# Second layer's attention: sums turned in the odd half, divided on VectorE; copies, statistics and norms moved

## What is computed

```
xn = layernorm(x);  x = x + attention0(xn) + ffn0(xn)   # 16 heads of 64; 32 experts, 6 taken
xn = layernorm(x);  x = x + attention1(xn) + ffn1(xn)   # below
```

## Time and profile before

| what | value |
|---|---|
| median of 3 runs | 1156.31 us (1155.72 to 1156.43) |
| the profiled execution | 1155.76 us |
| its span, first to last instruction | 1154.0 us |
| TensorE clock granted | 1.00 of full speed in every stage |
| second layer, group one / group two | about 939 to 1045 / 1045 to 1151 us of the span |
| rounds 1 to 4 of group one begin at | about 987, 1001.6, 1015.6 and 1029.9 us |
| rounds 1 to 4 of group two begin at | about 1092, 1106.2, 1120.3 and 1134.1 us |

### The profile page before, as it was taken

One profiled execution on the slowest core, in us unless ns is written; L12 is line 12 of the kernel. 1 busy time (PEld: TensorE's weight loads), 2 busy tenths in 40 slices (PEclk: granted clock), 3 DMA queues, 4 the chain that ended last, 5 costly groups with the idle time before them and its releaser, 6 DMA issues.

```text
span 1154.0 us, 24229 instructions
## 1 busy us (share of the span) xinstructions
PE 1139.0 (99%) x8984; PEld 897.8 (78%) x8984; DVE 998.3 (87%) x1917; ACT 839.7 (73%) x2240; POOL 484.9 (42%) x423
## 2 busy tenths in 40 slices
PE   8999999999999999999999999999999999999998
PEld 6778877877777787777778777877787767777776
DVE  7989798979897989898979897998888878898897
ACT  6886777577767775777577757776777757877886
POOL 2337600770077006700670067006750577735841
PEclk9999999999999999999999999999999999999999
DMA  8004101410041003101320032003300320000001
GB/s 270 2 32 145 49 1 31 138 57 1 31 139 55 1 31 129 66 1 31 129 65 1 25 129 71 2 18 129 119 1 9 136 87 1 2 21 19 2 11 28
DMA packets 44965, 63.93 MB, mean 55 GB/s; under 512 B 8240, under 2 KB 19120, under 8 KB 44592
## 3 DMA queue, kind: packets, MB, share of 16 engines
q1 hardware_dynamic: 44848, 62.39, 16.4%
HBM read 59.48 MB, written 2.88 MB: 54 GB/s over the span
## 4 chain that ended last, share of the span: by engine, by line
PE 90%; DVE 5%; ACT 2%; issue 1%; SPq 0%; DMA 0%; POOL 0%; DVEq 0%; ACTq 0%; POOLq 0%
PE psum L1730 14%; PE psum L1749 13%; PE psum L65 13%; PE psum L67 12%; PE psum L66 12%; PE psum L1671 11%; PE psum L1684 2%; PE psum L1696 2%; PE psum L2003 2%; PE psum L1753 1%; DVE mneg L1304 1%; PE psum L2059 1%; PE psum L1615 1%; ACT probs L876 1%; PE psum L2077 1%
## 5 line engine op out<-in xcount | busy, mean ns | idle before, releaser
L834 ACT ACTIVATE probs<-psum,mneg 128x256 f32<-128x256 f32 (+3 forms) x400 | 187.5, 486 | 109.6 <-DVE mneg L1285 109.0
L1730 PE MATMUL psum<-ident,probs 128*128 128x128 f32 x1600 | 210.1, 276 | 3.8 <-ACT probs L876 3.5
L1285 DVE TENSOR_REDUCE mneg<-psum 128x2 f32<-128x1024 f32 (+3 forms) x256 | 194.5, 818 | 21.4 <-PE psum L1684 17.5
L1276 DVE COPY pt<-psum 128x512 f32<-128x512 f32 x256 | 164.8, 683 | 41.5 <-PE psum L1730 39.5
L1730 PEld LDWEIGHTS psum<-ident,probs 128*128 128x128 f32 x1600 | 177.9, 141 | 28.4 <-ACT probs L834 8.2
L577 POOL TENSOR_TENSOR rstd<-var,mhalf 128x4 f32<-128x4 f32 x7 | 7.1, 1013 | 335.4 <-DVE var L1167 335.4
L1749 PE MATMUL psum<-pt,v_all 128*64 128x384 f32 (+5 forms) x1088 | 142.6, 412 | 0.0
L1749 PEld LDWEIGHTS psum<-pt,v_all 128*64 128x64 f32 (+1 forms) x1088 | 69.7, 135 | 62.7 <-issue 50.2
L65 PE MATMUL psum<-xt_hi,gu_hi 128*128 128x512 f32 x272 | 110.2, 405 | 0.0
L1363 DVE TENSOR_TENSOR sg<-sg,crow 128x512 f32<-128x512 f32 x88 | 106.1, 1206 | 3.6 <-DMA crow<-weights 0.9
L67 PE MATMUL psum<-xt_hi,gu_lo 128*128 128x512 f32 x272 | 107.7, 396 | 0.0
(11 more groups left out here) (307 smaller groups left out, 2895.2 us busy)
## 6 DMA issues: line engine op xcount, KB each, us to landing
crow<-weights SPq DMA_DIRECT2D x256, 128.0 KB, 2.9
rrow<-sums SPq DMA_DIRECT2D x128, 128.0 KB, 2.9
gu_raw<-in_gu SPq DMA_DIRECT2D x1, 2176.0 KB, 12.3
x_all<-in_x SPq DMA_DIRECT2D x7, 256.0 KB, 4.9
out_rows<-x_all SPq DMA_DIRECT2D x7, 256.0 KB, 2.3
down_raw<-in_down SPq DMA_DIRECT2D x1, 1088.0 KB, 13.4
wqkv_raw<-in_wqkv SPq DMA_DIRECT2D x1, 768.0 KB, 6.4
wqkv_raw<-in_wqkv SPq DMA_DIRECT2D x1, 512.0 KB, 4.0
```

The lines of the kernel that those rows point to most:

```text
L834: last = act.activation(probs[:, h * HALF + PROB[t]:h * HALF + PROB[t] + w], bank[score_bank(rnd, c) + h][:, o:o + w], ACT.Exp, bias=mneg[ ...
L1276: dve.tensor_copy(pt[:, s % 2, :, 3 - s // 2, :], turn_bank(rnd, s).rearrange("p (j q) -> p j q", q=P)).then_inc(pt_ready, 1)
L1285: last = dve.tensor_reduce(mneg_h[:, :, t], psum[:, b:b + 2, o:o + P * (t + 1)], AX, ALU.max, negate=True)
L1730: last = nc.tensor.transpose(dst[:, i * P:(i + 1) * P], probs[:, v:v + P], ident[:, :])
```

## The change

- PE: turn_sums1 moves from the end of the even half into the odd half, behind the odd pair's last scores, and into bank 7; the even pair's turn 4 goes to bank 6. output_rows moves behind turn 1 (second round) or turn 3 (third and fourth).
- DVE: in rounds two to four it divides, by multiplying the values in SBUF by the sums in bank 7 (divide), and leaves turn 2 of the even pair and turn 0 of the odd pair to ACT. In group one it takes turn 2 of the last odd pair itself again. add_attention moves behind turn 3 in the third and fourth rounds.
- ACT: the copy of the sums goes, except in the group's last batch; the two copies of turns come.
- POOL: the multiplication goes; in group one the first three normalised rows of the next group come, as a subtraction and a multiplication of 128x512 each, and the inverse roots of batches 6 and 7 stand together ahead of the first spread.
- Statistics: batch 6's on DVE go to the first layer's last batch, batch 7's to group one's first round, the first half between the copies and take_ffn, the second behind turn 1.
- Seam: turn 4 of the last odd pair is taken by DVE; PE's turn_sums1 there waits for add_attention of the third batch, no longer for turn 4's copy.

The diff, cut to its core (indentation reduced):

```diff
@@ -246,9 +246,10 @@
...
     return bank[[6, 2, 4, 3, 5][s]]
-return bank[([2, 3, 4, 7, 7] if k % (2 * G) else [6, 7, 0, 1, 7])[s]]
+return bank[([2, 3, 4, 7, 6] if k % (2 * G) else [6, 7, 0, 1, 7])[s]]
...
         SUMS = bank[5]
+        SUMS1 = bank[7]
@@ -738,6 +739,14 @@
...
 
+    def norm_rows1(g):
+        s = slice((n0 + G + g) * TILES, (n0 + G + g + 1) * TILES)
+        x = xn1[g]
+        pool.wait_ge(rows_ready, n0 + g + 1)
+        pool.wait_ge(x1_rstd_ready, n0 + G + g + 1)
+        setup.step(pool.tensor_tensor(x, x_all[:, n0 + G + g, :, :], mv[:, s, 0].unsqueeze(2).to_broadcast([P, TILES, D]), ALU.subtract))
+        pool.tensor_tensor(x, x, rstd[:, s].unsqueeze(2).to_broadcast([P, TILES, D]), ALU.mult).then_inc(row1_ready[g], 1)
+
@@ -774,14 +783,13 @@
...
         norm_qk(g)
+    if q + 1 < GROUPS:
+        inv_sqrt1(B - 2)
+        inv_sqrt1(B - 1)
...
         spread_sums1(n0 + g)
-        if q == 0 and 0 < g < G - 1:
-            inv_sqrt1(B - 3 + g)
-        if g < G - 1:
-            pool.wait_ge(rrow_ready, n0 + g + 1)
-            pool.wait_ge(y_ready, copied1(n0 + g + 1))
-            pool.tensor_tensor(y1t[g], y1t[g], rrow[:, 0, :], ALU.mult).then_inc(y_divided, 1)
+        if q + 1 < GROUPS and g:
+            norm_rows1(g - 1)
@@ -889,7 +897,7 @@
...
     act.wait_ge(y_divided, ROUNDS0 + n)
-    act.activation(rrow[:, 0, :], SUMS, ACT.Copy).then_inc(rrow_ready, 1)
+    act.activation(rrow[:, 0, :], SUMS1, ACT.Copy).then_inc(rrow_ready, 1)
@@ -1100,8 +1108,6 @@
...
             take_tile1_1(ka - 1)
-            if q == 0 and g > 1:
-                take_turned1(ka - 1, 2)
@@ -1118,13 +1124,16 @@
...
             copy_y1(g - 1)
-            take_sums1(n0 + g - 1)
-        if g:
+            take_turned1(ka, 2)
...
         exps1(kb, 1, 0)
+        if kb == 2 * B - 1:
+            take_turned1(kb, 0)
...
             take_tile1_1(ka)
+        elif kb < 2 * B - 1:
+            take_turned1(kb, 0)
@@ -1132,10 +1141,11 @@
...
             round_q(ROUNDS0 + n0 + g + 2, 1.0)
-    take_tile1_1(2 * (n0 + G) - 1)
...
         take_ht(q + 1, 0)
+    else:
+        take_tile1_1(2 * (n0 + G) - 1)
@@ -1257,8 +1267,9 @@
...
         variances0(b + 1)
-        if b:
-            add_row_stats(b - 1, x_all[:, b - 1, :, :])
+    if p == 7 and b:
+        dve.wait_ge(x1_ready, b)
+        add_row_stats(b - 1, x_all[:, b - 1, :, :])
@@ -1295,6 +1306,10 @@
...
         dve.tensor_copy(turned_rows1(k)[:, s % 2, :, 3 - s // 2, :], turn_bank1(k, s).rearrange("p (j q) -> p j q", q=P)).then_inc(pt1_ready[s], 1)
+
+def take_tile1_1(k):
+    dve.wait_ge(turned1[4], k + 1)
+    dve.tensor_copy(turned_rows1(k)[:, :, 0:2, 1, :], turn_bank1(k, 4).rearrange("p (h j q) -> p h j q", h=2, q=P)).then_inc(pt1_ready[4], 1)
@@ -1401,7 +1416,7 @@
...
             take_turned(n, [3])
-            if 0 < b < B - 1:
+            if b:
@@ -1520,6 +1535,11 @@
...
 
+    def divide(g, n0=n0):
+        dve.wait_ge(sums_turned, n0 + g + 1)
+        dve.wait_ge(y_ready, copied1(n0 + g + 1))
+        dve.tensor_tensor(y1t[g], y1t[g], SUMS1, ALU.mult).then_inc(y_divided, 1)
+
@@ -1529,8 +1549,7 @@
...
         if g:
-            if q or g == 1:
-                take_turned1(ka - 1, [2])
+            take_turned1(ka - 1, [2])
@@ -1539,10 +1558,13 @@
...
             row_maxima1(kb, 0)
-            take_turned1(ka, [1, 0, 2, 3])
+            take_turned1(ka, [1, 0, 3])
...
             take_turned1(ka, [0, 3])
+            if q == 0:
+                dve.wait_ge(x1_ready, B)
+                add_row_stats(B - 1, x_all[:, B - 1, :, :])
@@ -1552,7 +1574,9 @@
...
             invert_sums1(ka)
-        take_turned1(kb, [0])
+            take_turned1(kb, [0])
+        else:
+            divide(g - 1)
@@ -1561,18 +1585,15 @@
...
             row_maxima1(kb + 1, 0)
-        elif q + 1 < GROUPS:
-            dve.wait_ge(rows_ready, n0 + 1)
-            norm_rows1(n0 + G, 0)
-        if g:
+        if g == 1:
...
         take_turned1(kb, [1])
+        if q == 0 and g == 0:
+            sum_row_stats(B - 1, x1_var_ready)
...
         take_turned1(kb, [3])
-        if q == 0 and 0 < g < G - 1:
-            b = B - 3 + g
-            dve.wait_ge(x1_ready, b + 1)
-            row_stats(b, x_all[:, b, :, :], x1_var_ready)
+        if g > 1:
+            add_attention(g - 1)
@@ -1581,21 +1602,17 @@
...
         dve.wait_ge(y_done, ROUNDS0 + B + 1)
-        dve.wait_ge(rrow_ready, B)
+        dve.wait_ge(rrow_ready, GROUPS)
...
     take_turned1(2 * (n0 + G) - 1, [2])
-    dve.wait_ge(rows_ready, n0 + 2)
-    norm_rows1(n0 + G, 1)
-    if q + 1 < GROUPS:
-        dve.wait_ge(rows_ready, n0 + G - 1)
-        norm_rows1(n0 + G, G - 2)
-        stats1(q + 1, 0, 0)
+    take_tile1_1(2 * (n0 + G) - 1)
+    stats1(q + 1, 0, 0)
     dve.wait_ge(y_done, ROUNDS0 + n0 + G)
-    dve.wait_ge(rrow_ready, n0 + G)
+    dve.wait_ge(rrow_ready, q + 1)
@@ -1733,7 +1750,7 @@
...
     pe.wait_ge(spread_ready, n + 1)
-    transpose_rows(SUMS, spread).then_inc(sums_turned, 1)
+    transpose_rows(SUMS1, spread).then_inc(sums_turned, 1)
@@ -2066,7 +2083,7 @@
...
         elif q and g:
-            pe.wait_ge(rrow_ready, n0)
+            pe.wait_ge(rrow_ready, q)
@@ -2134,7 +2151,6 @@
...
     def output_rows(g, n0=n0):
-        pe.wait_ge(rrow_ready, n0 + g + 1)
@@ -2151,7 +2167,6 @@
...
         turn1(k, 1)
-        pe.wait_ge(pt1_ready[4], k)
@@ -2251,7 +2266,6 @@
...
         turn1(k, 2)
-        turn_sums1(n0 + g - 1)
@@ -2275,10 +2289,9 @@
...
         if g:
-            pe.wait_ge(pt1_ready[3], k)
+            pe.wait_ge(y_ready, copied1(n0 + g))
...
             pe.wait_ge(pt1_ready[2], k)
-            pe.wait_ge(rrow_ready, n0 + g)
@@ -2287,7 +2300,9 @@
...
         if g:
-            pe.wait_ge(y_ready, copied1(n0 + g - 1))
+            pe.wait_ge(pt1_ready[3], k)
+            turn_sums1(n0 + g - 1)
+            pe.wait_ge(pt1_ready[4], k)
@@ -2298,16 +2313,17 @@
...
             return
-        if g:
-            pe.wait_ge(pt1_ready[4], k)
-            output_rows(g - 1)
...
         turn1(k, 1)
+        if g == 1:
+            output_rows(g - 1)
...
         turn1(k, 3)
+        if g > 1:
+            output_rows(g - 1)
@@ -2330,7 +2346,7 @@
...
         break
-    pe.wait_ge(pt1_ready[4], 2 * (n0 + G))
+    pe.wait_ge(rows_ready, n0 + G - 1)
...
```

## The result

| what | before | after |
|---|---|---|
| median | 1156.04 us (1155.72 to 1156.69, 21 runs) | 1157.61 us (1157.06 to 1159.71, 21 runs) |
| the profiled execution, its span | 1155.76, 1154.0 us | 1157.61, 1155.8 us |
| after / before | | 1.0013, 95% interval 1.0007 to 1.0019 |

The change is slower by 1.6 us. This many runs tell the difference from zero, but it is only 0.13%, inside the 0.2% that the prediction counted as no change. The predicted time was 1156.8 us, in a range from 1153.8 to 1158.8.

The account below looks back on a forecast made before the run. PE was busy 1139.0 of 1154.0 us, DVE and ACT nearly full, ACT's slack against DVE 0.38 per round. Terms summed to +0.5: 1156.3 on the profiled execution, 1156.8 as median, range 1153.8 to 1158.8.

Parts of the forecast that it names:

- term 4: Group one's fourth round and the seam: PE's stop for DVE's normalised rows goes, POOL having them ready; -0.8 us.
- term 6: Group one's first round: batch 7's statistics delay ACT's first exponentials and, by their second half, turn 3's copy; +0.6 us.
- term 5: Group two's fourth round and end: 0.46 of sums, less 0.2 kept, plus 0.1 for the division; +0.3 us.
- Term 1: Group two's third round: ACT gates the odd scores, and its run with turn 0's copy delays the next scores; +0.1 us.
- Term 2: Group one's third round: batch 6's statistics leave DVE, turn 2's copy returns, round ends at 13.94; -0.3 us.
- Term 3: Second rounds, both groups: sums cost PE 0.46, new stop at turn 1 0.27, turn_k's stop shrinks; +0.3 us each.
- Term 7: POOL and first layer: inverse roots and spread hidden by 0.5, moved DVE work falls into idle time; no cost.
- Rival A: DVE was the bound: stops ending on it vanish with nothing late next; -3.3 us, 1153.0 us, chance 0.16.
- Rival B: ACT becomes the bound everywhere, its extra 0.48 paid five times; +2.6 us, 1158.9 us, chance 0.07.
- Rival C: First round: DVE's statistics are held beside POOL's long powers; 1.9 us added, 1158.7 us, chance 0.03.

Follow-up runs that it names:

- e2: The changed kernel plus one unused ACT copy of 128x512 behind the copy of the odd pair's turn 0, in five rounds; 1159.18 us, 1.0027.
- e6: The kernel before with only the statistics moved, both inverse roots ahead of the first spread, and turn 2 on DVE in every round; 1156.31 us, 1.0004.
- e4: The changed kernel with sums turned in the even half again and divided there by DVE, output_rows ahead of turn 1, odd pair's turn 0 on DVE; 1154.89 us.
- e7: The kernel before with only the normalised rows of the next group's first three batches on POOL; 1155.78 us, 1.0002.
- e8: e7 with the last odd pair's turn 4 copied by DVE ahead of turn 2, not by ACT; 1154.90 us, 0.9992 against the kernel before.
- e3: The changed kernel with the odd pair's turn 0 copied by DVE again, behind its division, not by ACT; 1157.19 us, 1.0012.
- e1: The changed kernel with batch 7's statistics moved into group one's feed-forward and between the first pair's copies of turns 0 and 3; 1156.38 us, 1.0004.
- e5: e4 with batch 7's statistics placed as in e1; 1154.33 us, 0.9986 against the kernel before.

## Why the prediction came out as it did

The forecast held: within 0.2%, the sign of the small rest included, and mostly for the reasons given. Two reasons were incomplete, those of term 4 and term 6. The time was 0.8 us low, and that it was not more is in part luck: the sum was set on 1156.31, the median of three runs, where 21 runs gave 1156.04. Against before, +0.5 was forecast and +1.57 and +1.10 measured in medians; by the ledger the work behind 980 us costs +1.12, so 0.6 was missing from the terms (0.26 of it in term 6, 0.15 in term 5), and what is above that varied between the two measurements of the same kernel.

**Term 1, third round, group two (+0.1): +0.12.** Step and reason held. The odd scores stand 0.24 behind ACT, and ACT's longer run decides the round's end. The traced execution was 1.29 late at the first scores of this round (1121.78 against 1120.49). Less this, ACT's run ended at 1134.16 and the next scores started at 1134.46, where 1134.19 and 1134.44 were forecast. e2 shows it from the other side, 0.52 for 0.52.

**Term 2, third round, group one (-0.3): -0.24.** e6 gives -0.39 without the longer ACT run, e2 +0.28 with one more copy.

**Term 3, second rounds (+0.3 each): +0.34 and +0.31.** The new stop ahead of turn 1 was there, and not among the waits: it lies inside a group. PE in group two's second round, against the earlier trace rows:

```profile
1116.62 0.65 PE L1632 MATMUL psum<-ident,crow 128*128 128x128 f32 x4
1117.12 1.31 PE L1747 MATMUL psum<-ident,probs 128*128 128x128 f32 x8
1118.26 1.06 PE L2157 MATMUL psum<-wo,v_all 128*128 128x128 f32 x8
1119.17 0.66 PE L1632 MATMUL psum<-ident,yt 128*128 128x128 f32 x4
...
1120.10 0.66 PE L1632 MATMUL psum<-ident,yt 128*128 128x128 f32 x4
```

Turns 0 and 1 together take 1.31, where eight matmuls without a stop take 1.04 to 1.06: 0.27, the forecast's number. turn_q stands at 1119.17 and turn_k at 1120.10; turn_k has no stop, where it had one of 0.31, or 0.47 by distances. e4, without the sums there, has +0.01.

**Term 4, the seam (-0.8): -0.72.** PE at the seam of the changed kernel, against the earlier trace rows:

```profile
1045.57 0.66 PE L1632 MATMUL psum<-ident,crow 128*128 128x128 f32 x4
1046.06 0.60 PE L1632 MATMUL psum<-ident,room 128*128 128x128 f32 x4
1046.50 0.38 PE L2018 MATMUL psum<-bias_bf,bias_on 96*128 96x512 bf16 x1
```

No stop is left. The size was right, one reason was missing: the forecast put the gain on POOL's rows, and e7 gives them nothing. The gain also needs turn 4's copy off ACT, which the forecast only priced as harmless. That the sum came right is luck in this point: the change does both. The seam itself is worth 1.04 (e8); the difference to 0.72 is what the fourth round loses, 0.25 of it to turn 0's copy on ACT (e3: -0.97).

**Term 5, fourth round of group two and end (+0.3): +0.45.** The forecast's own parts, 0.46 - 0.2 + 0.1, add up to 0.36 and were written as 0.3. PE in that round of the changed kernel:

```profile
1142.00 0.29 PE L1701 MATMUL psum<-hide,later 64*128 64x128 bf16 x4 [0.19 <-DVE pt L1308]
...
1144.53 0.66 PE L1632 MATMUL psum<-ident,crow 128*128 128x128 f32 x4
...
1145.98 1.16 PE L2157 MATMUL psum<-wo,room 128*128 128x128 f32 x8
```

The execution was 1.41 late at this round's first scores and 1.22 late at the masks of 1142.00 (1140.78 in before): 0.19 of the sums' place is kept, as forecast, and the stop for DVE's copy is what takes the rest. The sums then take 0.49 (to the next turn at 1145.02), and output_rows, which meets the division, takes 0.99 to the next turn at 1146.97, against 0.90 in before. The remaining 0.06 is spread over steps of 0.01 to 0.03. So each part was about right, and what was missing is the rounding and these small steps. e4, with +0.01, shows that all of it hangs on the sums' place and the edits that go with it.

**Term 6, first round (+0.6): +0.86.** The largest miss, in a term whose place was right: e6 and e1 show that the statistics are its whole cause. Its path was incomplete and one size too small. "The next maximum is late by only 0.4" was right: ACT began that chunk at 998.25, in before at 997.12, which is 0.39 more than the 0.74 by which this execution was late already. But the first exponentials, late by the whole 0.9, also gate PE's turns: they start at 998.22 against 996.57, 0.91 late, DVE's copy of a turn behind them is 0.87 late (999.32 against 997.71), and with it all that DVE does afterwards. DVE's idle time of 0.49 ahead of its inversion at 1000.58 in before then took part of the second half, which was 0.78 and not 0.56: 0.21 of this is in one instruction, nmean, 0.38 against the 0.17 of the same line at 981.12 in e1. e1 moved both halves at once, so how the 0.86 divides between them isn't shown.

**Term 7, POOL and first layer (0): held in size.** The spread of the second round was hidden, but by 1.0 and not by the 0.5 forecast: it ended at 1009.22 and DVE's inversion stood at 1010.24. The condition named, that without the first round's half microsecond DVE's next maxima would slip, did not come true: in e1 that cover is gone, the spread ended at 1008.43, the inversion stood at 1008.70 without a stop, and the round is +0.30 as in the changed kernel. What e5 met is another wait, which only the sums in the even half have: 0.54 of PE's time, ahead of the turn of the sums. The first layer costs nothing that can be seen: 0.05 and -0.05 at 980 us in the second trace of the changed kernel and in e1.

**Rival A** (DVE was the bound, -3.3) was right that DVE's stops at the ends of the odd halves, at turn_k and at the seam go, and fell as the forecast said: ACT was next at once. At the ends of the even halves DVE got six new stops. **Rival B** (ACT everywhere, +2.6) holds for the third rounds and group one's fourth, where one more copy came back whole (e2: 0.52, 0.52 and 0.50); the second rounds gave back half of it. **Rival C** (POOL holds the statistics, +1.9) fell: the first half took 0.86, beside a multiplication of two SBUF tensors on POOL and then beside the first of two powers of 2.27 each. The row that spoke against C was weak evidence, since POOL's copy lay beside only the first 0.2 of its 0.86. What was held was a small neighbour of theirs, for 0.21.

The lower end of the terms' own bounds, added by half, is 1155.45 and not 1155.2; nothing else was worked out from it.

## What to carry to other kernels

Where three queues are each over 80% full, what an instruction costs is decided by its place and not by its engine: the same sums, with the edits that go with them, cost 0.3 to 0.5 us a round in one half and nothing in the other (e4 against the changed kernel), and a copy moved between ACT and DVE changed the total by 0.1 us. Before an edit, look for the hole that it is to fill, and ask which of the other queues is within 0.3 us of being last; afterwards lay the two traces against each other instruction by instruction, since a stop can hide in a longer group. When one edit takes a delay away, look at what that delay had covered.

## What the runs showed of the hardware

A DVE tensor_scalar of four elements per partition took 0.38 us in the first round, beside POOL's multiplication of two SBUF tensors, and ended at 1002.44, as that one did (two of them from 1001.21 for 1.20: 1002.41). It did the same in e4 (0.41, ending at 1001.95, POOL's at 1001.93) and in e6 (0.39, ending at 1002.17, POOL's at 1002.15). In e1 the same line took 0.17 beside a POOL instruction as small as itself (981.05, 0.20), and for batch 7 it took 0.27, ending at 993.44 with a POOL multiplication that ended at 993.41. The Trainium skill (SBUF — State Buffer, section "SBUF: two separate sides") says that VectorE and GpSimd share a port pair which one of them holds for a whole instruction while the other waits. The trace agrees, and shows it for an instruction of this size: priced by its own length it is too cheap by the rest of POOL's.

The statistics were not slowed: 0.86 at 994.83, as in the earlier trace rows. POOL's multiplication of two SBUF tensors ran beside them until 995.37, and its long power, which rival C feared, from 995.33 on. Nor was the aggregation of 0.37 slowed at 1001.65, beside the multiplication that held its neighbour; in the earlier trace rows's batch it took 0.38.

An ACT copy of 128x512 from PSUM took 0.48 from start to start and DVE's 0.60, so a copy handed from DVE to ACT costs the receiver less than it spares the giver.
